# Edge aggregation on one core: 5 of the 17 edge tiles of a group multiplied whole in fp32

## The chip, the cores and the metric

The kernel runs on one core of one Trainium2 chip. The metric is the device time of one execution in microseconds (us). Engines are named as the profile names them: PE is TensorE, DVE VectorE, ACT ScalarE, POOL GpSimd, SP SyncE. A name with a q behind it (ACTq) is that engine's sequencer, the part that loads registers, branches, waits for semaphores and issues DMAs.

## The reference

Two GraphSAGE layers over a graph of 6250 nodes, 100000 edges (sorted by target `dst`) and 512 features, then a mixture of 8 experts with the best 2 for each node:

```python
def _sage_layer(h, src, dst, W_self, W_neigh, b, n_nodes):
    agg = segment_sum(h[src], dst, num_segments=n_nodes)
    deg = segment_sum(ones_like(dst), dst, num_segments=n_nodes)
    h_neigh = agg / maximum(deg, 1.0)[:, None]
    return relu(h @ W_self + h_neigh @ W_neigh + b)

h = _sage_layer(_layernorm(x), src, dst, W_self1, W_neigh1, b1, n)     # layer 1
h = _sage_layer(h, src, dst, W_self2, W_neigh2, b2, n)                 # layer 2
x = x + h
x = x + moe(_layernorm(x))                    # top 2 of 8 experts, 512 -> 512 -> 512
```

## The kernel before

**Stages.** First x is normalized into HBM (`xn_scratch`, about the first 108 us), and beside that DVE and PE make small tables from the edge list (`tables`, `in_order`, `tables2`, `tables3`). Then come layer 1, layer 2 and the experts.

**A layer.** The edges stand in 784 tiles of 128 edges (782 with real edges; `ET`, `TT`). POOL issues one indirect DMA for each tile (`gather`, L685) that fetches the 128 source rows into one of 28 slots of `store_all`. The nodes are done in 49 groups of 128. A group steps through 17 edge tiles (`ST`), k = 0 to 16, that start at its first tile; a tile that holds edges of two groups is stepped through in both. The rest of a group, seldom there, runs in an inner loop (k = 17). The sum over edges is a product with a 0/1 matrix: `sel` (edges x nodes of the group, built by DVE for three tiles at a time, L1232) times the rows.

**The split.** The rows are fp32 and are multiplied as two fp32r products. ACT rounds them to fp32r (`half`, L834, writes `r_hi`), DVE subtracts (`other_half`, L1240, writes `r_lo`), and PE multiplies `sel` by both (`sums`, L1646 and L1647); in layer 1 a third, 2 columns wide, counts the degree (L1645). `r_hi`, `r_lo` and `sel` are rings of 6 tiles: ACT and DVE wait for PE's semaphore `seg` before they write into a ring place again (`free_at`).

**Order.** `layer` writes the same order of steps on PE, ACT and DVE: before step k the pieces in `hooks[k]` are done, which belong to the node work of the group before or the one before that. On PE these are the 8 dense pieces of 3 matmuls at k = 0, 2, ... 14 (L1619), transposes at 3 and 11, and in layer 2 also transposes at 5, logits at 9, the list product at 13 and prefix sums at 17. On ACT `relu` (layer 1, L902) stands at 17 and waits for the last dense piece. In 32 of the groups of layer 1 (4 to 35) ACT also moves the experts' weights: `store_split` at 17 (L874), `load_raw` at 0 (L868). At the start of each group every engine loads its table entries into registers (`value`, L375): `tab_tile` on all three, and `tab_pos` on ACT alone (`places`).

**Slots.** SP passes on the arrival of each gather (`arrived`, L571). Every fourth tile it also waits until DVE's count `lo` (tiles whose `r_lo` is done) has passed the tiles 17 to 20 back (`freed`, L581), and then frees 4 slots; POOL waits for that before the gather that goes into them (L582 names it in the profile).

**Unsorted edges.** Where the tables find that the edges are not sorted (`loose`), every group goes over all 784 tiles again (`tab_laps`, `tab_pos`). With this input that path is not taken, but its table work and its loads are done.

## Time and profile before

| what | value |
|---|---|
| median of 3 runs | 3189.15 us (3183.64 to 3189.4) |
| profiled execution: own time / span | 3192.86 us / 3191.1 us |
| PE busy, weight loads busy | 2713.7 us (85%), 2108.6 us (66%) |
| DVE, ACT, POOL busy | 2280.9 (71%), 1727.3 (54%), 2189.5 us (69%) |
| granted PE clock, mean of the span | 0.904 |
| layer 1, from the first gather to the first of layer 2 | 108.9 to 1260.5 us |
| layer 2, to the end of its gathers | 1260.5 to 2371 us |

The span is what the profile shows between the first and the last instruction; the execution's own time is 1.8 us more. A busy share is an average over stages with different limits, and the ends of matmuls are modelled, so two matmuls in a row overlap in the rows; the distance between their starts is what one costs.

### The profile page before, as it was taken

How to read it: one execution, taken by the hardware profiler on the slowest of the kernel's cores; microseconds unless marked ns; L12 is line 12 of the kernel's file. 1: busy time of each engine (PE TensorE's matmuls, PEld its weight loads, DVE VectorE, ACT ScalarE, POOL GpSimd, SP SyncE). 2: the span in 40 equal slices, each digit the busy share in tenths (PEclk: the TensorE clock that was granted, in tenths of full speed). 3: DMA queues.
4: the chain of work that ended last, by engine and by line, in shares of the span. 5: the costliest groups of instructions: out<-in, count | busy, mean ns of one | idle time of the engine just before them, and what ended most of it. 6: DMA issues, size and time to landing. Idle time of an engine off the chain costs nothing.

```text
span 3191.1 us, 66577 instructions
## 1 busy us (share of the span) xinstructions
PE 2713.7 (85%) x12191; PEld 2108.6 (66%) x12192; DVE 2280.9 (71%) x5226; ACT 1727.3 (54%) x3193; POOL 2189.5 (69%) x2216
## 2 busy tenths in 40 slices
PE   1488878887889987899999999999996999899997
PEld 0366666666667765677777677777774777777775
DVE  7567666766667775888888888888875666666665
ACT  3455545545556654655656566555553555555554
POOL 0577777777777776777777777777753556555665
PEclk9988888888889998989899899888887999999998
DMA  7788888778877776777777777777765554555443
GB/s 276 230 256 267 270 273 268 254 254 267 257 247 227 213 215 222 231 231 231 235 236 234 234 230 234 227 233 224 235 196 157 136 135 75 132 133 135 73 80 63
DMA packets 234835, 664.22 MB, mean 208 GB/s; under 512 B 46602, under 2 KB 48196, under 8 KB 227612
## 3 DMA queue, kind: packets, MB, share of 16 engines
q0 software_dynamic: 151712, 465.58, 52.3%
q10 hardware_dynamic: 60768, 127.43, 11.2%
q1 hardware_dynamic: 22300, 70.69, 6.1%
q14 instruction: 46, 0.38, 0.0%
q8 instruction: 9, 0.15, 0.0%
HBM read 551.72 MB, written 111.83 MB: 208 GB/s over the span
## 4 chain that ended last, share of the span: by engine, by line
PE 36%; POOL 28%; issue 12%; DMA 11%; ACTq 5%; DVE 4%; ACT 2%; SPq 2%; DVEq 1%; POOLq 0%
POOL store_all L685 27%; PE ps L1619 22%; PE ps L1646 6%; DMA store_all<-h_scratch,srcT 5%; PE ps L1647 4%; ACTq L375 2%; DMA out<-store_all,idx_s 2%; DMA store_all<-xn_scratch,srcT 2%; DVE r_lo L1240 1%; PE ps L1747 1%; PE ps L1759 1%; DMA m_g<-gate_scratch,idx_g 1%; ACT r_hi L834 1%; ACTq L874 1%; ACTq L868 1%
## 5 line engine op out<-in xcount | busy, mean ns | idle before, releaser
L834 ACT ACTIVATE r_hi<-store_all 128x512 fp32r x1680 | 1008.0, 626 | 747.0 <-SPq L571 406.0
L1240 DVE TENSOR_TENSOR r_lo<-store_all,r_hi 128x512 fp32r<-128x512 f32 x1680 | 1130.2, 687 | 344.7 <-ACT r_hi L834 339.7
L685 POOL DMA_INDIRECT store_all<-xn_scratch,srcT x784 | 863.2, 1101 | 274.1 <-issue 227.4
L685 POOL DMA_INDIRECT store_all<-h_scratch,srcT x784 | 872.8, 1113 | 254.2 <-issue 239.3
L1646 PE MATMUL ps<-r_hi,sel 128*128 128x512 f32 x1680 | 831.0, 495 | 94.9 <-DVE r_lo L1240 94.0
L1647 PE MATMUL ps<-r_lo,sel 128*128 128x512 f32 x1680 | 711.2, 423 | 0.0
L1646 PEld LDWEIGHTS ps<-r_hi,sel 128*128 128x128 f32 x1680 | 348.4, 207 | 229.7 <-DVE r_lo L1240 162.1
L1232 DVE TENSOR_TENSOR sel<-iota_g,dstT 128x384 fp32r (+4 forms) x602 | 317.9, 528 | 137.3 <-PE ps L1647 93.8
L1619 PE MATMUL ps<-wts,sT 128*128 128x512 f32 x1176 | 415.7, 469 | 0.0
L1647 PEld LDWEIGHTS ps<-r_lo,sel 128*128 128x128 f32 x1680 | 352.5, 210 | 21.7
L1645 PEld LDWEIGHTS ps<-ones_col,sel 128*128 128x128 f32 x840 | 173.5, 206 | 286.7 <-issue 155.1
L1619 PE MATMUL ps<-wts,m_hT 128*128 x1224 | 326.4, 417 | 27.8 <-DVE m_hT L1496 23.3
L1645 PE MATMUL ps<-ones_col,sel 128*128 128x2 f32 x840 | 164.3, 196 | 209.2 <-DVE r_lo L1240 208.6
L1619 PE MATMUL ps<-wts,aT 128*128 128x512 f32 x1176 | 336.4, 395 | 0.0
L1619 PEld LDWEIGHTS ps<-wts,sT 128*128 128x128 f32 x1176 | 257.6, 227 | 86.8 <-issue 29.7
L1619 PE MATMUL ps<-wts,m_xT 128*128 x1224 | 311.6, 403 | 2.6 <-DVE m_xT L1486 2.5
L1619 PEld LDWEIGHTS ps<-wts,m_hT 128*128 128x128 f32 x1224 | 231.8, 196 | 98.4 <-issue 47.4
L1619 PEld LDWEIGHTS ps<-wts,m_xT 128*128 128x128 f32 x1224 | 223.2, 189 | 49.9 <-issue 3.4
L1619 PEld LDWEIGHTS ps<-wts,aT 128*128 128x128 f32 x1176 | 220.3, 188 | 52.6 <-DVE aT L1263 0.5
L953 ACT ACTIVATE store_all<-ps,b1T 128x128 f32<-128x128 f32 x408 | 116.7, 369 | 238.1 <-PE ps L1759 238.1
L743 POOL DMA_INDIRECT out<-store_all,idx_s x102 | 165.4, 1622 | 109.3 <-DMA store_all<-xn_scratch,idx_x 90.7
L730 POOL DMA_INDIRECT store_all<-xn_scratch,idx_x x104 | 105.6, 1015 | 121.4 <-PE ps L1747 87.2
(283 smaller groups left out, 3120.3 us busy)
## 6 DMA issues: line engine op xcount, KB each, us to landing
expert_weights_scratch<-w_both ACTq DMA_DIRECT2D x64, 512.0 KB, 5.2
wts<-expert_weights_scratch SPq DMA_DIRECT2D x32, 1024.0 KB, 10.3
store_all<-in_L_ffn_W ACTq DMA_DIRECT2D x64, 256.0 KB, 5.4
self_t<-xn_scratch ACTq DMA_DIRECT2D x49, 256.0 KB
store_all<-xn_scratch,srcT POOLq DMA_INDIRECT x784, 3.9
h_scratch<-x_t ACTq DMA_DIRECT2D x49, 256.0 KB
self_t<-h_scratch ACTq DMA_DIRECT2D x49, 256.0 KB
store_all<-h_scratch,srcT POOLq DMA_INDIRECT x784, 4.0
```

Of the source, the lines that this page charges most:

```text
L375: return eng.value_load(cell, min_val=0, max_val=top)
L685: pool.indirect_dma_start(rows[:, t % SLOTS, :], None, rows_d, bass.IndirectOffsetOnAxis(ap=srcT[:, t:t + 1], axis=0)).then_inc(s_rows[t % ...
L730: pool.indirect_dma_start(m_x, None, xn2_d, bass.IndirectOffsetOnAxis(ap=idx_x[:, 0:1], axis=0)).then_inc(M["x"], 16)
L743: pool.indirect_dma_start(out, bass.IndirectOffsetOnAxis(ap=idx_s[:, 0:1], axis=0), m_y, None, compute_op=ALU.add).then_inc(M["scat"], 16)
L834: act.activation(r_hi[:, ring(k), :], slot_of(t), ACT.Copy) \
L953: i = act.activation(m_hr[:, k, :], mhT_p[:, k * P:(k + 1) * P], ACT.Relu, bias=bias)
L1232: dve.tensor_tensor(sel[:, a:a + w, :], of_tile(g).unsqueeze(1).to_broadcast([P, w, P]), dstT[:, bass.ds(t, w)].unsqueeze(2).to_broadcast( ...
L1240: dve.tensor_tensor(r_lo[:, ring(k), :], slot_of(t), r_hi[:, ring(k), :].bitcast(F32), ALU.subtract).then_inc(S["lo"] if k < ST else S["lo ...
L1619: i = pe.matmul(out_ap, lhs[:, a, k, :], w[:, b, k, :], start=start and k == chunks[0] and (a, b) == (0, 0), stop=stop and k == chunks[-1] ...
L1645: pe.matmul(deg_of(g), sel[:, a, :], ones_col[:], start=k == 0, stop=False)
L1646: pe.matmul(agg_of(g), sel[:, a, :], r_hi[:, a, :], start=k == 0, stop=False)
L1647: pe.matmul(agg_of(g), sel[:, a, :], r_lo[:, a, :], start=False, stop=False) \
```

## The change

- `WHOLE = (2, 5, 8, 11, 14)`: for these 5 of the 17 steps ACT makes no `r_hi` and DVE no `r_lo`. PE multiplies `sel`, read as fp32, by the gathered rows in their slot as one fp32 matmul. It waits for `sel` (new semaphore) and for the arrival of the rows (`arr`). The inner loop (k = 17) stays split. The counts of `hi` and `lo` go by 12 tiles a group.
- Slots are freed by PE's `seg` (tile multiplied) and not by DVE's `lo` (tile split).
- The path for unsorted edges is gone: `in_order`, the `loose` steps of `tables2`, `tab_pos`, `tab_laps`, one product and one transpose of PE. 782 gathers a layer are issued and not 784.
- The last group covers nodes 6144 to 6249 alone: its edges are looked for from 6144 on (`thr_lo`), and the rows it shares with the group before are not stored by it (`own_rows`).

```diff
+WHOLE = (2, 5, 8, 11, 14)
+NSPLIT = ST - len(WHOLE)
+NSEL = -(-ST // SELW)
...
-                if places:
-                    t0 = value(eng, cell(places, g), NT * ET)
...
-                sp.wait_ge(S["lo"], packed // PACK + lap * ST)
-                sp.wait_ge(S["lox"], packed % PACK + lap * (ET - ST) + 1)
+                sp.wait_ge(S["seg"], packed // PACK + RING)
+                sp.wait_ge(S["segx"], packed % PACK + 1)
                 sp.sem_inc(S["slot"], BATCH)
...
-                for t in range(ET):
+                for t in range(TT):
...
                 def half(k, g, x, t):
 
+                    if k in WHOLE:
+                        return
...
-                layer(act, half, hooks, tab_tile, places=tab_pos, loop_end=loop_end,
+                layer(act, half, hooks, tab_tile, loop_end=loop_end,
...
-                        dve.wait_ge(S["lo"], g * ST)
+                        dve.wait_ge(S["sel"], g * NSEL)
...
+                        if k < ST:
+                            built.then_inc(S["sel"], 1)
+
+                    if k in WHOLE:
+                        return
                     if k < ST:
-                        dve.wait_ge(S["hi"], g * ST + (k + 1))
+                        dve.wait_ge(S["hi"], g * NSPLIT + (split_no(k) + 1))
...
                 def sums(k, g, x, t):
                     a = ring(k)
 
+                    if k in WHOLE:
+                        pe.wait_ge(S["sel"], g * NSEL + (k // SELW + 1))
+                        alone(pe, S["arr"], t + 1)
+                        if l == 0:
+                            pe.matmul(deg_of(g), sel[:, a, :], ones_col[:], start=False, stop=False)
+                        pe.matmul(agg_of(g), sel[:, a, :].bitcast(F32), slot_of(t), start=False, stop=False) \
+                            .then_inc(S["seg"], 1)
+                        return
```

PE in layer 1, steps k = 1 and 2 of a group and the piece at 3 (s1_ is a semaphore of layer 1), before:

```order
L1645 MATMUL ps<-ones_col,sel 128x2 [waits s1_lo]
L1646 MATMUL ps<-r_hi,sel 128x512
L1647 MATMUL ps<-r_lo,sel 128x512
L1619 MATMUL ps<-wts,sT 128x512 x3
L1645 MATMUL ps<-ones_col,sel 128x2 [waits s1_lo]
L1646 MATMUL ps<-r_hi,sel 128x512
L1647 MATMUL ps<-r_lo,sel 128x512
L1666 MATMUL ps<-ident,agg_s 128x128 [waits s1_aggLo,s1_evac]
```

and the same place after the change (L1584 is the dense piece, L1639 the transpose):

```order
L1618 MATMUL ps<-ones_col,sel 128x2 [waits s1_lo]
L1619 MATMUL ps<-r_hi,sel 128x512
L1620 MATMUL ps<-r_lo,sel 128x512
L1584 MATMUL ps<-wts,sT 128x512 x3
L418 ISA [waits s1_sel]
L1609 MATMUL ps<-ones_col,sel 128x2 [waits s1_arr]
L1610 ISA
L1610 MATMUL ps<-store_all,sel 128x512
L1639 MATMUL ps<-ident,agg_s 128x128 [waits s1_aggLo,s1_evac]
```

Step 2 no longer waits for DVE's `lo`, and one matmul of 512 columns that reads the slot itself stands where two stood.

ACT in layer 1 in the loop that also moves the experts' weights, from the start of a group (`load_raw` is L868) to its first step, before:

```order
L375 TENSOR_LOAD tab_tile
L375 ISA x2
L375 REGISTER_ALU
L375 TENSOR_LOAD tab_pos
L375 ISA x2
L425 REGISTER_ALU [waits s_wset]
L868 ISA [waits s_wl]
L868 DMA store_all<-in_L_ffn_W 128x512 x2
```

and after the change, where `load_raw` is L856:

```order
L368 TENSOR_LOAD tab_tile
L368 ISA x2
L418 REGISTER_ALU [waits s_wset]
L856 ISA [waits s_wl]
L856 DMA store_all<-in_L_ffn_W 128x512 x2
```

The second register load, of `tab_pos`, is gone from ACT's start of a group.

## Rows read from the trace of the kernel before

**Rows 1.** Busy time by stretch: us, each engine (instructions), granted clock, DMA, GB/s.
```profile
228.00:986.00 758.00, 614.41 (x2684) 484.43 (x2684) 506.40 (x908) 396.68 (x687) 567.59 (x514) 0.85 0.82 263
986.00:1060.00 74.00, 71.23 (x346) 56.70 (x345) 59.93 (x112) 47.47 (x85) 57.85 (x54) 0.98 0.72 217
1290.00:2376.00 1086.00, 1005.96 (x4519) 776.58 (x4519) 909.62 (x2345) 639.75 (x1105) 849.72 (x763) 0.90 0.75 230
```

**Rows 2.** Line L1653, PE, one a group: ns min/median/max, first, last start.
```profile
L1653 PE MATMUL ps<-zero_row,zero x31: 245/245/348, 252.0 to 985.5; 2*128 2x2 f32 x31
...
L1653 PE MATMUL ps<-zero_row,zero x4: 245/245/245, 1003.6 to 1059.4; 2*128 2x2 f32 x4
...
L1653 PE MATMUL ps<-zero_row,zero x48: 266/266/368, 1309.8 to 2376.0; 2*128 2x2 f32 x48
```

**Rows 3.** The chain of waits, 490 to 510 us: start us, us, what.
```profile
495.98 0.71 PE ps L1619 x3
...
498.58 1.38 ACTq L375
...
500.29 0.62 ACTq L375
...
504.39 0.37 PE ps L1645
```

**Rows 4.** Waits, 229 to 986.5 us: who <- for whom, us, times, longest us.
```profile
PE ps L1645 <- DVE r_lo L1240: 143.0, 36, 5.3
```

**Rows 5.** Waits, 1290 to 2377 us.
```profile
ACT r_hi L834 <- SPq L571: 299.4, 381, 4.9
...
PE ps L1646 <- DVE r_lo L1240: 75.3, 121, 1.6
```

**Rows 6.** Register loads by line L375, 229 to 986.5 us: ns min/median/max.
```profile
L375 ACTq TENSOR_LOAD <-tab_pos x32: 272/666/970, 229.8 to 985.1; - x32
```

**Rows 7.** PE in order of time, layer 1: start us, us, what.
```profile
1011.61 0.16 PE L1645 MATMUL ps<-ones_col,sel 128*128 128x2 f32 x1
...
1012.18 0.17 PE L1645 MATMUL ps<-ones_col,sel 128*128 128x2 f32 x1
```

**Rows 8.** PE in order of time, layer 2.
```profile
2018.13 0.40 PE L1647 MATMUL ps<-r_lo,sel 128*128 128x512 f32 x1
...
2018.60 0.39 PE L1647 MATMUL ps<-r_lo,sel 128*128 128x512 f32 x1
```

**Rows 9.** PE in order of time, the table products.
```profile
56.55 2.77 PE L1612 MATMUL ps<-ident,need 112*1 112x112 f32 x14 [6.47 <-DVE need L1157]
```

**Rows 10.** PE in order of time, the first edge tiles.
```profile
123.96 0.63 PE L1647 MATMUL ps<-r_lo,sel 128*128 128x512 f32 x1
124.38 0.20 PE L1645 MATMUL ps<-ones_col,sel 128*128 128x2 f32 x1
```

**Rows 11.** Line L685, POOL, the gathers: ns min/median/max, first, last start.
```profile
L685 POOL DMA_INDIRECT store_all<-xn_scratch,srcT x784: 950/957/2684, 108.9 to 1243.8; - x196
L685 POOL DMA_INDIRECT store_all<-h_scratch,srcT x784: 950/963/2233, 1260.5 to 2370.6; - x196
```

**Rows 12.** DVE and POOL in order of time, 114 to 118 us.
```profile
114.95 4.49 DVE L393 TENSOR_TENSOR wts<-store_all,wts 128x2048 fp32r<-128x2048 f32 x2 [20.11 <-ACT wts L388]
115.39 2.68 POOL L685 DMA_INDIRECT store_all<-xn_scratch,srcT  x1 [0.30 <-issue]
```

**Rows 13.** Waits of SP's sequencer, 229 to 986.5 us.
```profile
SPq L581 <- DVE r_lo L1240: 270.6, 92, 8.2
```

**Rows 14.** Page part 5: busy us, mean ns of one, idle before.
```profile
L1240 DVE TENSOR_TENSOR r_lo<-store_all,r_hi 128x512 fp32r<-128x512 f32 x1680 | 1130.2, 687 | 344.7 <-ACT r_hi L834 339.7
...
L1232 DVE TENSOR_TENSOR sel<-iota_g,dstT 128x384 fp32r (+4 forms) x602 | 317.9, 528 | 137.3 <-PE ps L1647 93.8
```

**Rows 15.** DVE in order of time, table work.
```profile
50.70 0.23 DVE L1134 TENSOR_SCALAR lap_row<-iota,loose 1x49 f32<-1x49 f32 x1
...
51.71 0.51 DVE L1145 TENSOR_TENSOR ahead<-tid,ps 112x343 f32<-112x343 f32 x1
```

## What the change does to the time, forecast before it was run

> **What bounds the kernel now.** I read the busy time by stretch first [rows 1]. Layer 1 has two regimes. Up to 986 us PE is 81% busy at a granted clock of 0.85; from 986 to 1060 us it is 96% busy at 0.98. Layer 2 lies between, 93% at 0.90. POOL is busy 75 to 78% in all three, but each gather is followed by 0.30 us of its own sequencer [rows 12], so POOL has almost nothing left either: 0.96 + 0.30 = 1.26 us is the least a gather takes, and layer 2 spends (2370.6 - 1260.5) / 783 = 1.42 us on one [rows 11].
>
> The period of a group comes from the start of its closing matmul [rows 2]. Up to 986 us it is (985.5 - 252.0) / 30 = 24.45 us, from 1003.6 to 1059.4 it is 18.6 us, and in layer 2 (2376.0 - 1309.8) / 47 = 22.7 us. A group needs about 16 new tiles (782 / 49), so the gathers alone would ask for 16 x 1.42 = 22.7 us. That is layer 2 exactly: there ACT waits 299 us for arrivals [rows 5], the gathers bound it, and PE follows with 75.3 / 48 = 1.6 us of waiting for `r_lo` a group. The 18.6 us is what PE needs when tiles lie ready and the clock is up: the price of a group on PE.
>
> The long periods up to 986 us are neither. The chain of waits shows them [rows 3]: PE ends the last dense piece (495.98 + 0.71), ACT's `relu` follows, ACT issues the stores of the split weights, loads `tab_tile` (1.38 us) and `tab_pos` (0.62 us), issues the loads of raw weights, rounds tile 0, DVE subtracts, and only at 504.39 can PE start tile 0. For some 4.6 us of it PE stands (143.0 us in 31 groups) [rows 4]. Everything else in that period is PE going from tile 0 to the last dense piece without a pause. PE also pulls the gathers back: SP waits 270.6 us for the split tiles before it frees slots [rows 13]. So in this region, about 33 groups with those before 252 us, each microsecond of PE work between tile 0 and the last dense piece counts in full.
>
> **One whole tile on PE.** At full clock a tile of layer 1 takes 12.18 - 11.61 = 0.57 us from start to start [rows 7], of layer 2 2018.60 - 2018.13 = 0.47 us [rows 8]. For a 512-column fp32 matmul the trace has no row; the nearest are the 7 table products with 112 columns, which are recorded as 14 [rows 9]: an fp32 matmul is two passes in the record, each 0.18 to 0.20 us long, 1.6 to 1.8 ns a column. The split matmul beside it takes 124.38 - 123.96 = 0.42 us for 512 columns, 0.82 ns each, at the half clock (0.63 us long there, 0.40 in rows 8) [rows 8, 10]. So a pass of fp32 costs twice a column and there are two: four fp32r matmuls for two. At full clock that is 4 x 0.21 to 0.23 = 0.87 us for 0.46, +0.41 us a tile; at half clock +0.86 us. Lower bound: no more than the pair it replaces, 0. Upper bound: if the table products ran at full clock, 2 x 512 x 1.77 ns = 1.8 us, +1.35 us. I take +0.41, since PE had been idle for 6.5 us before them, and the split matmuls that start after an idle time run at half clock [rows 9, 10].
>
> **Layer 1 up to 986 us.** Whole tiles 2, 5, 8 and 11 stand between tile 0 and the last dense piece (at k = 14); tile 14 stands behind it, beside ACT's chain, and is free while ACT takes longer. Tile 2 comes right after the stall, at half clock. That is 0.86 + 3 x 0.41 = 2.1 us a group. Against it ACT's chain loses `tab_pos`: its median is 0.67 us in this stretch [rows 6], with the 0.2 us of register work behind it 0.87 us, say 0.9. Net +1.2 us, times 33: **+40 us**. It could be 0, if the shorter stall keeps PE's clock up (2.1 us less half of a colder time of 3 to 4 us, less 0.9), and +76, if two more of the whole tiles fall into half clock. What ACT and DVE save there (5 x 0.63 and 5 x 0.69 us a group) is hidden by PE.
>
> Slots are now freed when PE is done with a tile, not DVE, which runs up to 6 ring places ahead. While PE bounds it this shifts nothing, but at 986 us up to 5 fewer gathers are under way: +5 us (0 to 8).
>
> **Gathers.** Their median is 0.96 us and the longest 2.7 us [rows 11]. The row at 115.39 shows what stretches them: that gather began while DVE ran the first of two subtractions with both operands in SBUF (4.49 / 2 = 2.2 us each, so until 117.2), and ended 0.9 us behind it, 1.7 us later than a usual one [rows 12]. In layer 2 a gather loses 1.42 - 0.96 - 0.30 = 0.15 us, over 1566 gathers some 235 us. By busy time r_lo has 1130 / (1130 + 318) = 0.78 of it against `sel` [rows 14], 183 us, and 490 of the 1680 r_lo go: 53 us, 0.034 us a gather. Between 0 (nothing of it is r_lo's) and 0.05. This counts only where gathers bound: the last 184 of layer 1 (783 less those issued by 986 us), **-6 us**; two empty gathers less at the end of layer 1, 2 x 1.4 = **-3 us**.
>
> The Trainium skill, page "SBUF — State Buffer", section "Who interferes with whom", says otherwise: a VectorE instruction with two SBUF inputs holds up a GpSimd instruction that reads SBUF, not one that only writes, and `tensor_tensor` did not stall descriptor generation. By that rule the term of -6 us would be 0 and the gather-bound case below would lose its gain. The row at 115.39 speaks against it, 2.68 us where 0.96 is usual [rows 11, 12].
>
> **Layer 2.** PE gets 5 x 0.41 = 2.05 us more a group, 2.5 with the fifth of the time that it spends at half clock [rows 1]. It has 1.6 us of waiting to put it in [rows 5], and less waiting should give back some of the clock; each 0.01 of clock is about 0.2 us. 22.7 - 1.6 + 2.5 - 0.6 = 23.0 us, against gathers of 16 x (1.42 - 0.034) = 22.2. PE becomes the bound there, by +0.3 us x 48 = **+15 us**; between -30 (gather-bound, see below) and +45 (no clock given back).
>
> **Start.** The table steps that go stand in DVE's chain ahead of the first gather: 51.71 - 50.70 = 1.0 us for one run of six [rows 15], and about 12 more of 0.15 to 0.5 us; together **-3 us** (0 to -5, as loads of x may fill it). Loads, stores and experts: no term, PE bounds the experts and nothing there is changed. The stores of the last group are 22 rows shorter, nothing.
>
> **Sum.** +40 +5 -6 -3 +15 -3 = +48 us on the profiled execution's own 3192.86 us gives 3241. That execution lies 3.7 us above the median of the runs, 3189.15, so the forecast is 3189 + 48 = **3237 us**. Its own range is 3192 to 3285: the first term between 10 and 60 us and layer 2 between 0 and 40.
>
> **Rivals.**
>
> *The gathers stay the bound (faster).* With fewer waits PE's clock rises and 2 us a group fit in. The Trainium skill, page "TensorE: Matmul & The Clock Gate", section "Why this matters for your kernels", asks for TensorE to be busy without gaps to keep the full clock; rows 1 agree as far as 0.98 in the dense stretch. Then layer 2 follows the gathers, 784 x -0.034 - 3 = -30 us, layer 1 up to 986 us is even, its end -9 and the start -3: -42 us, 3147 us. Against it: in layer 2 PE needs 18.6 + 2.05 = 20.7 us at full clock, but there are also small matmuls (logits, prefix sums) after which rows of before show the clock down.
>
> *PE pays more (slower).* The clock gives nothing back and half of the whole tiles up to 986 us meet the half clock: 33 x (3.2 - 0.9) = +76, layer 2 +45, slots +5, the rest -12: +114 us, 3303 us. It decides from the point where PE's period in layer 2 passes 23.5 us. For it: the mean clock of 0.85 [rows 1] leaves three tenths of the time at half speed.
>
> *An fp32 matmul costs no more than the pair.* Then ACT's saving stays (-30), gathers give -30 and the rest -9: -69 us, 3120 us. Only the short width of the table products leaves room for it.
>
> *The change does nothing*, since gathers bound before and after and PE absorbs it: within 6 us of before. It needs the gains and the losses of the first case to cancel.
>
> **How the numbers follow.** Chances: the forecast 0.62, PE pays more 0.18, gathers bound 0.12, fp32 cheap 0.03, nothing 0.05. What can be told from no change is about 0.2%, 6 us: below 3183 is faster, above 3195.5 slower. The forecast and the case above it are slower but for 0.04 of the forecast's low end, 0.76; faster 0.15; the same 0.09. For 8 in 10 the range runs from 3170, which leaves out most of the two fast cases, to 3300, which leaves out the upper half of the dear one.
>
> **What would show it.** The whole matmul in two records of about 0.43 us from start to start at full clock; the period of a group up to the end of the weights' moving at 25.6 us, and in layer 2 at 23.0 with PE over 97% busy and ACT's waits for arrivals well below 299 us; the register load of `tab_pos` gone from the chain; gathers with a mean 0.03 us shorter; SP waiting for PE where it freed slots. The forecast is wrong if the period in layer 2 is 22.2 us or less, or if the records of the whole matmul are much shorter or longer than 0.43 us.

## The result and the profile after

The changed kernel took 3151.28 us (median of 4 runs, 3146.70 to 3156.34), the kernel before on the same chip 3187.41 us (4 runs): a ratio of 0.9885, interval 0.9869 to 0.9901. It is faster by 36 us; 3237 us and "slower" were forecast. The profiled execution took 3153.0 us, its span 3151.2 us, 39.9 us under that of before.

Where the 39.9 us came from is read from the closing matmuls (now L1626), one a group. Groups 5 to 35 are the early stretch of layer 1 (closing 4 to closing 35), closings 49 to 97 are layer 2:

```profile
L1626 PE MATMUL ps<-zero_row,zero x32: 245/245/348, 223.8 to 982.8; 2*128 2x2 f32 x32
...
L1626 PE MATMUL ps<-zero_row,zero x49: 265/266/267, 1286.4 to 2339.5; 2*128 2x2 f32 x49
```

Before, the same closings stood at 228.1, 985.5, 1289.5 and 2376.0 (two of them in [rows 2]). So the start gave 4.3 us, the early stretch lost 1.5 (757.5 to 759.0), closings 35 to 49 gave 0.4, **layer 2 gave 33.4** (1086.5 to 1053.1), and what follows gave 3.4. The last of these is not read as a gain: what follows layer 2 took between 811.7 and 816.2 us in the kernels of the table below, with no edit to it among e1 to e16. The early stretch, where +40 was forecast, didn't move; layer 2, where +15 was forecast, is the gain.

The stretches of [rows 1] after the change, by stretch: us, each engine (instructions), granted clock, DMA share, GB/s:

```profile
228.00:983.00 755.00, 656.15 (x2678) 470.73 (x2678) 414.64 (x753) 313.03 (x532) 534.87 (x507) 0.91 0.81 261
983.00:1060.00 77.00, 77.00 (x348) 56.02 (x348) 48.68 (x93) 37.26 (x65) 59.88 (x57) 1.00 0.73 220
1290.00:2340.00 1050.00, 1020.16 (x4510) 741.26 (x4508) 785.52 (x2105) 496.03 (x864) 803.87 (x758) 0.95 0.77 237
```

The granted clock rose from 0.85 to 0.91 and from 0.90 to 0.95. In layer 2 PE is 97% busy, yet it is not the bound. The chain of waits of layer 2 (start us, us, what) is one gather behind another, each with its 0.30 us of sequencer, for tens of microseconds on end:

```profile
2010.24 0.95 POOL store_all L687
2011.19 0.30 issue
2011.49 0.95 POOL store_all L687
2012.44 0.30 issue
```

ACT still waits for arrivals, less than the 299.4 us of [rows 5] (who <- for whom: us, times, longest us), and PE waits less for `r_lo`: its matmuls for `r_lo` (75.3 us in [rows 5]) are no longer among the longest waits, only its weight loads:

```profile
ACT r_hi L822 <- SPq L569: 218.4, 194, 5.8
...
PEld ps L1619 <- DVE r_lo L1208: 56.5, 94, 1.7
```

The gathers that set the pace are shorter. Of line L687 the page gives the count, the busy us and the mean ns (1113 for layer 2 before); the view of the line gives ns min/median/max, where [rows 11] had a longest one of 2233 ns:

```profile
L687 POOL DMA_INDIRECT store_all<-h_scratch,srcT x782 | 828.9, 1060 | 262.0 <-issue 225.9
```

```profile
L687 POOL DMA_INDIRECT store_all<-h_scratch,srcT x782: 949/956/1498, 1257.6 to 2323.7; - x196
```

The whole tile itself costs what was forecast. PE in order of time, layer 2 (start us, us, what): from the first of the two records of the fp32 matmul to the next operation it is 0.86 us, where a split tile of [rows 8] took 0.47. The second fence is the chain of waits of an early group: it has 0.97 us for a layer-1 tile with its degree matmul, where [rows 7] had 0.57:

```profile
1690.67 1.02 PE L1610 MATMUL ps<-store_all,sel 128*128 x2
1691.53 0.95 PE L1672 MATMUL ps<-wg_s,store_all 128*128 128x8 f32 x8
```

```profile
494.25 1.39 ACTq L368
495.67 0.15 ACTq L368
...
499.19 0.37 PE ps L1618
...
502.86 0.97 PE ps L1610 x2
```

The second load of [rows 3] is gone: one `L368` stands there. PE's wait for the first tile's `r_lo`, 143.0 us in [rows 4], is 99.7 us. SP waits for PE where it frees slots (299.1 + 125.4 us in the early stretch, against 270.6 for DVE in [rows 13]).

### The profile page after: what moved, and what is told of

Its sections match the earlier page's. It is cut to its first block, busy times and chain, and to the rows that moved or that the text cites. A ratio compares the mean times of both kernels' runs of the same rounds, so it can differ in the third digit from the quotient of the medians.

```text
span 3151.2 us, 64888 instructions
## 1 busy us (share of the span) xinstructions
PE 2786.8 (88%) x12188; PEld 2058.8 (65%) x12189; DVE 2007.8 (64%) x4721; ACT 1446.7 (46%) x2703; POOL 2109.5 (67%) x2212
## 3 DMA queue, kind: packets, MB, share of 16 engines
q10 hardware_dynamic: 60660, 127.29, 11.1%
## 4 chain that ended last, share of the span: by engine, by line
PE 48%; POOL 22%; issue 10%; DMA 9%; ACTq 4%; DVE 3%; ACT 2%; DVEq 1%; SPq 1%; POOLq 0%
PE ps L1584 24%; POOL store_all L687 22%; PE ps L1610 6%; PE ps L1619 6%; PE ps L1620 4%; DMA out<-store_all,idx_s 2%; DMA store_all<-h_scratch,srcT 2%; ACTq L368 1%; DVE r_lo L1208 1%; PE ps L1720 1%; PE ps L1732 1%; DMA m_g<-gate_scratch,idx_g 1%; DMA store_all<-in_x 1%; DMA store_all<-xn_scratch,srcT 1%; ACT r_hi L822 1%
## 5 line engine op out<-in xcount | busy, mean ns | idle before, releaser
L687 POOL DMA_INDIRECT store_all<-xn_scratch,srcT x782 | 824.3, 1054 | 304.3 <-issue 223.4
L822 ACT ACTIVATE r_hi<-store_all 128x512 fp32r x1190 | 721.3, 626 | 660.4 <-SPq L569 318.8
L687 POOL DMA_INDIRECT store_all<-h_scratch,srcT x782 | 828.9, 1060 | 262.0 <-issue 225.9
L1208 DVE TENSOR_TENSOR r_lo<-store_all,r_hi 128x512 fp32r<-128x512 f32 x1190 | 804.8, 687 | 303.6 <-ACT r_hi L822 301.5
L1619 PE MATMUL ps<-r_hi,sel 128*128 128x512 f32 x1190 | 582.4, 489 | 44.6 <-DVE r_lo L1208 44.1
L1610 PE MATMUL ps<-store_all,sel 128*128 x980 | 540.4, 634 | 0.0
L1620 PE MATMUL ps<-r_lo,sel 128*128 128x512 f32 x1190 | 493.8, 415 | 0.0
L1584 PE MATMUL ps<-wts,sT 128*128 128x512 f32 x1176 | 424.9, 474 | 0.0
L1584 PE MATMUL ps<-wts,aT 128*128 128x512 f32 x1176 | 374.7, 427 | 0.0
L1584 PE MATMUL ps<-wts,m_hT 128*128 x1224 | 327.1, 418 | 23.8 <-DVE m_hT L1464 20.7
L1619 PEld LDWEIGHTS ps<-r_hi,sel 128*128 128x128 f32 x1190 | 238.8, 201 | 156.3 <-DVE r_lo L1208 81.9
L1584 PEld LDWEIGHTS ps<-wts,sT 128*128 128x128 f32 x1176 | 240.7, 212 | 113.8 <-issue 70.8
L1584 PE MATMUL ps<-wts,m_xT 128*128 x1224 | 312.1, 404 | 2.5 <-DVE m_xT L1454 2.5
L1584 PEld LDWEIGHTS ps<-wts,m_hT 128*128 128x128 f32 x1224 | 232.9, 197 | 93.9 <-issue 42.2
L1584 PEld LDWEIGHTS ps<-wts,aT 128*128 128x128 f32 x1176 | 221.2, 188 | 88.7 <-issue 45.8
L1618 PEld LDWEIGHTS ps<-ones_col,sel 128*128 128x128 f32 x595 | 118.7, 199 | 221.8 <-issue 129.6
L1620 PEld LDWEIGHTS ps<-r_lo,sel 128*128 128x128 f32 x1190 | 242.0, 203 | 24.1 <-issue 9.4
L1584 PEld LDWEIGHTS ps<-wts,m_xT 128*128 128x128 f32 x1224 | 224.0, 190 | 49.6 <-issue 3.4
```

The source lines that it names most:

```text
L687: pool.indirect_dma_start(rows[:, t % SLOTS, :], None, rows_d, bass.IndirectOffsetOnAxis(ap=srcT[:, t:t + 1], axis=0)).then_inc(s_rows[t % ...
L822: act.activation(r_hi[:, ring(k), :], slot_of(t), ACT.Copy) \
L1208: dve.tensor_tensor(r_lo[:, ring(k), :], slot_of(t), r_hi[:, ring(k), :].bitcast(F32), ALU.subtract).then_inc(S["lo"] if k < ST else S["lo ...
L1584: i = pe.matmul(out_ap, lhs[:, a, k, :], w[:, b, k, :], start=start and k == chunks[0] and (a, b) == (0, 0), stop=stop and k == chunks[-1] ...
L1610: pe.matmul(agg_of(g), sel[:, a, :].bitcast(F32), slot_of(t), start=False, stop=False) \
L1618: pe.matmul(deg_of(g), sel[:, a, :], ones_col[:], start=k == 0, stop=False)
```

## The experiments

Each stretch below is read from the closings of the kernel's own trace, the gathers from its page. "Early" is closings 4 to 35, "layer 2" closings 49 to 97. Each ratio is to the kernel before on the same chip. The ratios are of medians, the other columns of one profiled execution each, which lies up to 6 us from its kernel's median (e8: 14 us above it). How far a stretch varies where nothing in it was changed is seen in e1, e5 and e6, whose layer 1 is the same: 743.9, 738.2 and 741.4 us in the early stretch, and 1053.8, 1050.6 and 1055.4 us from closing 4 to 49. Differences of under 6 us between single stretches are not read as effects.

| kernel | ratio (interval) | early, us | layer 2, us | gather in layer 2, mean / longest ns |
|---|---|---|---|---|
| before | 1 | 757.5 | 1086.5 | 1113 / 2233 |
| the change | 0.9885 (0.9869 to 0.9901) | 759.0 | 1053.1 | 1060 / 1498 |
| e1, no whole tile | 0.9981 (0.9969 to 0.9992) | 743.9 | 1093.9 | 1120 / 2236 |
| e2, TensorE's part alone | 1.0037 (1.0022 to 1.0053) | 767.0 | 1092.2 | 1112 / 2232 |
| e3, relief without price | 0.9830 (0.9805 to 0.9855) | 750.7 | 1050.2 | 1061 / 1891 |
| e4, change + load | 1.0075 (1.0053 to 1.0096) | 811.9 | 1052.3 | 1064 / 1500 |
| e5, layer 2 only | 0.9857 (0.9838 to 0.9877) | 738.2 | 1052.7 | 1063 / 1499 |
| e6, seven in layer 2 | 0.9947 (0.9931 to 0.9964) | 741.4 | 1082.7 | 1023 / 1480 |
| e7, two-input filler | 1.0011 (1.0001 to 1.0021) | 763.8 | 1094.0 | 1114 / 2238 |
| e8, one-input filler | 1.0003 (0.9991 to 1.0015) | 766.7 | 1098.8 | 1125 / 2007 |
| e13, ScalarE kept busy | 0.9907 (0.9890 to 0.9924) | 766.1 | 1052.2 | 1063 / 1499 |
| e14, small filler | 0.9860 (0.9845 to 0.9874) | 757.7 | 1055.9 | 1064 / 1497 |
| e15, e1 + slots by `r_lo` | 0.9966 (0.9954 to 0.9978) | 740.7 | 1087.3 | 1112 / 2234 |
| e16, e1 + load | 1.0015 (1.0005 to 1.0025) | 757.8 | 1093.6 | 1120 / 2252 |

**e1, no whole tile.**

```
-WHOLE = (2, 5, 8, 11, 14)
+WHOLE = ((), ())          # one list a layer
```

> The change without its whole tiles: all 17 edge tiles of a group are split again, in both layers; the freed slots, the shorter tables, the removed position load and the removed path stay. Two theories of the 36 us that the change gained. Theory R (relief): with five r_lo fewer in a group, VectorE holds up fewer gathers, they stay the bound of layer 2 and are shorter, and TensorE's extra time fits beneath. Then the whole tiles bring nearly all of it: this run takes 3180 to 3190 us, its layer-2 period is 22.6 to 22.8 us and a gather lasts 1.10 us again. Theory L (load): the terms of the forecast for the removed load (33 groups x 0.9 us) and for the start hold, and it is they that paid: this run takes 3150 to 3160 us, with the early groups at 23.0 us instead of 23.9. The third, theory C (clock), says that the denser TensorE gives half-clock time back: this run is then near 3185 us too, but with half-clock time in layer 2 again at 4 to 5 us a group.

3186.81 us, ratio 0.9981. All else of the change is worth 6 us, the whole tiles some 30 (0.9981 to 0.9885). Theory L falls: the 14 us won in the early stretch (757.5 to 743.9) are lost again later (closings 35 to 49: 304.0 to 309.9 us, layer 2 +7.4). Layer 2 is slow again with long gathers. Its rows (closings; then the two stretches, as above):

```profile
L1626 PE MATMUL ps<-zero_row,zero x49: 266/266/369, 1278.2 to 2372.1; 2*128 2x2 f32 x49
```

```profile
224.40:968.30 743.90, 628.47 (x2683) 497.07 (x2683) 510.76 (x908) 399.01 (x687) 573.71 (x512) 0.86 0.83 267
...
1278.20:2372.10 1093.90, 1021.82 (x4521) 794.20 (x4520) 910.66 (x2347) 638.29 (x1106) 852.48 (x760) 0.88 0.75 228
```

**e2, TensorE's part alone.** The early returns for whole tiles are taken out on ScalarE and VectorE; PE waits for an `r_lo` that it doesn't read.

```
                     if k in WHOLE:
                         ...
+                        pe.wait_ge(S["lo"], g * ST + k + 1)
                         ...
                         pe.matmul(agg_of(g), sel[:, a, :].bitcast(F32), slot_of(t), start=False, stop=False) \
```

> The five tiles are multiplied whole on TensorE, but ScalarE and VectorE still make r_hi and r_lo for all 17 (the five halves are made and not used), so no engine but TensorE is changed by the whole tiles. Theory R: no relief, the gathers stay at 1.10 us and the layer-2 period at 22.7 us or above, TensorE pays what it can't hide: 3185 to 3230 us. Theory C: the fuller TensorE keeps its clock without any relief: 3150 to 3170 us, layer-2 period near 22.0 us.

3207.81 us, ratio 1.0037: slower than before, in theory R's range. Layer 2 took 1092.2 us, as without whole tiles, so nothing is gained (theory C falls, as the cause of the gain), and nothing is lost either: PE took in the five whole tiles. The rows show how:

```profile
227.50:994.50 767.00, 663.58 (x2682) 474.02 (x2683) 510.51 (x908) 401.74 (x687) 548.56 (x512) 0.91 0.81 259
...
1300.60:2392.80 1092.20, 1046.81 (x4521) 747.04 (x4520) 908.27 (x2347) 637.28 (x1106) 846.94 (x761) 0.95 0.76 229
```

In layer 2 PE's 240 whole tiles cost 240 x 0.39 = 94 us at full clock. PE's busy time rose by 25 us only (1021.8 to 1046.8), while the granted clock rose from 0.88 to 0.95, so some 69 us came back from the clock. The other kernels that split all tiles (before, e15, e16) have 1006.2 to 1011.1 us at 0.89 to 0.90; against them it is 36 to 41 us more and 53 to 58 back. In the early stretch the price is 31 groups x 5 x 0.40 = 62 us, and PE's busy time rose by 35 us at a clock of 0.91 instead of 0.86: at most 27 us came back there, and the stretch lengthened by 23 us.

**e3, relief without price.**

```
-                        pe.matmul(agg_of(g), sel[:, a, :].bitcast(F32), slot_of(t), start=False, stop=False) \
+                        pe.matmul(agg_of(g), sel[:, a, :], slot_of(t).bitcast(F32R), start=False, stop=False)
+                        pe.matmul(agg_of(g), sel[:, a, :], slot_of(t).bitcast(F32R), start=False, stop=False) \
```

This kernel leaves out the rest of the rows (`r_lo`) and counts them twice in these tiles; it serves for the time alone.

> The other half: ScalarE and VectorE are spared the five tiles as in the change, but TensorE multiplies the row itself twice in fp32r (as long as a split tile takes; the sums of these five tiles come out doubled), so TensorE pays nothing. Theory R: the relief alone is the gain, the whole tiles' price was hidden in layer 2 and partly paid in layer 1: 3120 to 3150 us, layer-2 period 21.9 us as with the change, TensorE idle more. Theory C: without a fuller TensorE the clock falls again, and the time is above the change's, 3160 to 3185 us, with 4 to 5 us at half clock in a layer-2 group.

3143.23 us, ratio 0.9830. The relief alone has the whole gain of layer 2 (1050.2 us) at a clock of 0.91. So a higher clock isn't what gains; it is what pays for the whole tiles.

**e4, the load again.**

```
                 packed = value(eng, cell(table, g), ET * PACK + ET)
                 ...
+                if last == 2:              # ScalarE in layer 1
+                    value(eng, cell(tab_extra, g), NT * ET)
```

> The change, with one more register load for each group on ScalarE where the removed position load stood (of the table of further tiles, its value unused). The forecast's term says 0.9 us a group in the early region of layer 1, some 30 us in all: 3175 to 3185 us. If the load stood beside other waits there it costs under 0.2 us a group: 3148 to 3156 us.

3218.47 us, ratio 1.0075, some 61 us above the change (0.0190 x 3193). The early stretch took 811.9 us, 52.9 more, 1.7 us a group; the forecast had 0.9. The chain of waits of an early group (start us, us, what): the second load and its register work put 1.3 us between the first and everything behind:

```profile
514.83 0.94 ACTq L368
515.80 0.15 ACTq L368
516.10 0.94 ACTq L368
517.06 0.15 ACTq L368
517.60 0.36 ACTq L858
```

The stretch's clock fell from 0.91 to 0.87 with it. PE waits 33.6 us longer for the first tile (99.7 to 133.3 us), and its busy time is 20 us longer (657.4 to 677.7).

```profile
225.50:1037.40 811.90, 677.66 (x2683) 482.99 (x2683) 416.52 (x753) 313.46 (x531) 539.30 (x511) 0.87 0.77 244
```

**e5 and e6, layer 2 only; seven tiles.** `WHOLE` becomes one list a layer.

```
+WHOLE = ((), (2, 5, 8, 11, 14))          # e5
+WHOLE = ((), (2, 4, 6, 8, 10, 12, 14))   # e6
```

> The five whole tiles in layer 2 alone; layer 1 splits all 17. Theory R (relief, pays where the gathers set the pace): layer 2 keeps its 1053 us (closings 49 to 97, against 1094 us without whole tiles), and layer 1 no longer pays for the whole tiles: its end stands as without them, 8 us earlier than with the change. That gives 3140 to 3148 us at this chip's pace of the first runs. If the layers weren't separate (layer 1's whole tiles also pay), it is at the change's 3151 us or above.

3147.64 us beside 3196.80 of before, 0.9857. Layer 2 keeps its gain (1052.7 us), and layer 2 begins 11.1 us earlier than with the change (1275.3 against 1286.4). The intervals of the two ratios overlap, so that it beats the change by some 9 us is likely, not shown by the medians.

> Seven whole tiles (2, 4, ..., 14) in layer 2, none in layer 1. Theory R gives 8.2 us for each r_lo spared in layer 2 (41 us for five) as long as TensorE fits beneath: a group at full clock is 20.46 us with five, 21.3 us with seven, and the gathers' pace would be 21.6 us: 3124 to 3132 us. If the gathers' gain is no longer had (TensorE sets the pace once waits and some half-clock time are added), the layer stays at 1050 us or above and the time at 3140 us or above.

3178.54 us, 0.9947: the second case. The gathers are shorter still (1023 ns), but POOL now waits 55.0 us for slots (11.9 with the change), SP waits for PE where it frees them, and PE is busy for 98% of layer 2 at 0.95; seven whole tiles make it the bound. The stretch, and SP's waits in it:

```profile
1278.70:2361.40 1082.70, 1059.56 (x4522) 747.07 (x4521) 732.10 (x2011) 450.22 (x771) 777.79 (x761) 0.95 0.76 231
```

```profile
SPq L578 <- PE ps L1620: 409.3, 95, 9.3
...
SPq L578 <- PE ps L1610: 152.4, 45, 7.0
```

**e7 and e8, fillers on VectorE.**

```
                     if k in WHOLE:
+                        dve.wait_ge(s_fixed, g * len(WHOLE) + (l * NT * len(WHOLE) + WHOLE.index(k) + 1))
+                        dve.tensor_tensor(fixed[:, 1], fixed[:, 0], fixed[:, 0], ALU.subtract).then_inc(s_fixed, 1)
                         return
```

and in e8, in place of the last added line:

```
+                        dve.tensor_scalar(fixed[:, 1], fixed[:, 0], 1.0, None, ALU.add).then_inc(s_fixed, 1)
```

> The change, but VectorE does for each whole tile, in the place of the r_lo that it is spared, a subtraction of the same size with two inputs in SBUF, of a constant (its result isn't used). ScalarE and TensorE stay as changed. If it is VectorE's two-input operations that hold up the gathers, the relief is gone: layer 2 at 1085 to 1100 us, a gather at 1.10 us, 3185 to 3205 us. If it is ScalarE's r_hi that was the load on them, or only that VectorE and ScalarE free their buffers sooner, it stays at 3150 to 3160 us.

3199.19 us, 1.0011; layer 2 at 1094.0 us, gathers at 1114 ns. VectorE's work is the cause, as expected.

> As the run before, with an operation that reads one input (a constant plus 1.0, same 128x512 size) in place of the subtraction. If the gathers are held up by two-input operations alone, this one costs next to nothing: 3148 to 3160 us, a gather at 1.05 to 1.06 us, layer 2 at 1053 us. If any work of VectorE on SBUF holds them up, it is as slow as with the subtraction, in proportion to its length.

3197.89 us, 1.0003; layer 2 at 1098.8 us. This is against what I expected: a filler with one input, 0.44 us long (0.69 for the other), costs as much. So "two inputs" is not the whole of it. The profiled execution is the slowest of its 12, 14 us above the median, so its layer 2 may be some us too long; the ratio says the same without it.

**e9 to e12 and e17, e18: two slower chips.** Six kernels fell on two chips where the kernel before itself took 3801 and 3783 us, not 3193 to 3197. In layer 2 of the change there (e17) POOL waited for free slots for 313.5 us, where it waited for 11.9 on the first chip (POOL's waits: us, times, longest us):

```profile
POOL store_all L687 <- SPq L579: 313.5, 100, 11.0
POOL store_all L687 <- issue: 200.6, 647, 1.0
```

The DMA engines moved 185 GB/s in that stretch there, 237 on the first chip. Why is open: these traces don't say when a gather landed. Another thing than the gathers' issue bounds there (layer 2 took 1321 to 1341 us in all six), so four of them were repeated (e13 to e16). Their edits and those of the repeats are the same.

> The change, but ScalarE makes for each whole tile a copy of the size of an r_hi, of a constant (not used), behind the same two waits; VectorE stays relieved. Theory V: the gain of layer 2 is VectorE's alone: layer 2 stays at 1050 to 1060 us and the time at 3148 to 3162 us. If ScalarE's relief carried part of it, layer 2 rises toward the 1092 us of the run with both halves kept.

3698.36 us, ratio 0.9756 (0.9706 to 0.9807).

> The run with VectorE's one-input filler cost layer 2 as much as the two-input one (1099 and 1094 us), against what I expected. This one has the same 490 fillers on 32 columns instead of 512. Theory O (occupancy: what counts is how long VectorE works without a hole, since a gather that starts in a hole is not held): a filler of some 100 ns gives most of the gain back, layer 2 at 1053 to 1065 us, 3150 to 3170 us in all. Theory I (one more instruction with its wait between the r_lo shifts what each gather meets, whatever its length): layer 2 stays at 1085 us or above.

3681.76 us, 0.9721 (0.9667 to 0.9775).

> No whole tiles, and the slots are freed by r_lo (before TensorE has multiplied) as in the kernel before, not by TensorE. The forecast's term says that freeing by TensorE costs 5 us, all of it in the early groups of layer 1: this run is then 5 us below the one without whole tiles, at 0.9965 of before. If later freeing costs nothing, as layer 2 suggests (no wait for slots there), it is within 2 us of it, 0.998.

3747.74 us, 0.9850 (0.9778 to 0.9921).

> No whole tiles, and the extra register load on ScalarE again: near to the kernel before in all but the freed slots. The load cost 62 us beside the whole tiles, where the forecast had 0.9 us for each of 33 groups. If the load's price depends on the whole tiles (TensorE's later r_hi), it is far cheaper here, 10 to 30 us: 1.001 to 1.008 of before. If it is the load itself (1.27 us of ScalarE's queue ahead of the copy of the sums in each early group), it costs 50 us or more here too: 1.013 or above.

3650.13 us, 0.9627 (0.9577 to 0.9677): the fastest of the six, with no whole tile and one load too many. None of the four forecasts came true there, and none of these runs answers its question. For the last pair see the end of this section.

**e13, ScalarE kept busy.** In `half`, for a whole tile, behind the same waits:

```
+                        act.activation(fixed[:, 1], fixed[:, 0], ACT.Copy).then_inc(s_idle, 1)
```

> The kernel with ScalarE kept busy (a copy of a constant for each whole tile, VectorE relieved), again, since the last call's chip had slow transfers (before at 3801 us; the gathers no longer set the pace alone). Theory V, VectorE's relief alone pays: layer 2 at 1050 to 1060 us, ratio to before 0.988 to 0.991. If ScalarE's relief carries part of it: layer 2 toward 1092 us, ratio above 0.994.

3165.39 us, 0.9907; layer 2 at 1052.2 us. The gain of layer 2 is VectorE's alone. The early stretch is 7 us longer (766.1 against 759.0), little more than it varies by; that ScalarE's work does it is not shown.

**e14, small filler.** As e8, on 32 columns (0.19 us).

> The filler of 32 columns on VectorE, again. Theory O (occupancy): layer 2 at 1053 to 1065 us, ratio 0.988 to 0.993. Theory I (an instruction more, whatever its length): layer 2 at 1085 us or above, ratio 0.998 or above.

3152.27 us, 0.9860; layer 2 at 1055.9 us. These fillers' number and waits don't matter; how long VectorE works does. Theory O's forecast came true, though between 0.19 us (no cost) and 0.44 us (the whole cost) nothing was tried.

**Why a gather is held.** The traces of e1 and e8 say what e8 left open. VectorE and POOL in order of time in layer 2, first of e1, then of the change (start us, us, what):

```profile
2011.89 0.48 DVE L1352 TENSOR_SCALAR w_both<-iota_c,col_f,idcode 128x400 fp32r<-128x400 f32 x1
2012.04 2.23 POOL L687 DMA_INDIRECT store_all<-h_scratch,srcT  x1 [0.30 <-issue]
2012.29 0.56 DVE L1196 TENSOR_TENSOR sel<-iota_g,dstT 128x384 fp32r x1
2012.76 0.69 DVE L1208 TENSOR_TENSOR r_lo<-store_all,r_hi 128x512 fp32r<-128x512 f32 x1
```

```profile
2011.49 0.95 POOL L687 DMA_INDIRECT store_all<-h_scratch,srcT  x1 [0.30 <-issue]
2011.58 0.69 DVE L1208 TENSOR_TENSOR r_lo<-store_all,r_hi 128x512 fp32r<-128x512 f32 x1
...
2015.01 0.68 DVE L1208 TENSOR_TENSOR r_lo<-store_all,r_hi 128x512 fp32r<-128x512 f32 x1
...
2015.26 1.25 POOL L687 DMA_INDIRECT store_all<-h_scratch,srcT  x1 [0.30 <-issue]
```

A gather that begins in a hole of VectorE takes 0.95 us, even if an `r_lo` begins 0.09 us behind it: of 494 such gathers in both layers of the change one was held. One that begins inside an `r_lo` ends 0.82 us behind its end (2015.69 to 2016.51). Of 500 that began inside an `r_lo`, 369 took over 1.00 us. What is left of the `r_lo` decides: with 0.2 us or more left 347 of 368 were held, with less than 0.13 us none of 57. That is the usual 0.95 less the 0.82: the place in the issue where it is held lies some 0.13 us behind its start (an estimate from these rows).

An unbroken row of operations doesn't hold a gather to its end as such. In the change a gather that begins inside `sel`, with an `r_lo` right behind, ends 0.82 us behind `sel` (2018.67 to 2019.49):

```profile
2018.11 0.56 DVE L1196 TENSOR_TENSOR sel<-iota_g,dstT 128x384 fp32r x1
2018.22 1.27 POOL L687 DMA_INDIRECT store_all<-h_scratch,srcT  x1 [0.31 <-issue]
2018.58 0.68 DVE L1208 TENSOR_TENSOR r_lo<-store_all,r_hi 128x512 fp32r<-128x512 f32 x1
```

So did all 134 that were held of the 187 that began that way, and all 65 held of 66 that began in an `r_lo` with another behind. The long ones begin inside an operation with one input, `w_both` in the rows of e1, with `sel` and `r_lo` right behind, and end 0.82 us behind the `r_lo`: 2.23 us. All 38 over 1.9 us in layer 2 of e1 are of this kind; of the 48 with e8's kernel 17 are, and 31 begin where the filler and a short `place_i` end:

```profile
2003.09 0.42 DVE L1208 TENSOR_SCALAR fixed<-fixed 128x512 f32<-128x512 f32 x1
2003.42 0.16 DVE L1338 CAST place_i<-place 128x2 int32<-128x2 f32 x1
2003.47 2.00 POOL L689 DMA_INDIRECT store_all<-h_scratch,srcT  x1 [0.30 <-issue]
2003.49 0.55 DVE L1200 TENSOR_TENSOR sel<-iota_g,dstT 128x384 fp32r x1
2003.96 0.68 DVE L1214 TENSOR_TENSOR r_lo<-store_all,r_hi 128x512 fp32r<-128x512 f32 x1
```

Why a gather that begins in the operation ahead is held through two, and one that begins in the first of the two only through one, stays open.

The last column of the table splits the kernels in two by the long ones: 1.5 us where five or seven `r_lo` are spared without a long filler (1.9 in e3), 2.0 or more elsewhere. Gathers over 1.9 us number 38 in layer 2 of e1, 26 before, 32 with e2's and e7's kernels each and 48 with e8's; there is none in layer 2 of the change and none with the small filler.

By what runs when the held gather begins, the time above 0.953 us of gathers over 1.00 us in layer 2 is:

| begins inside | e1 | the change | e7 | e8 |
|---|---|---|---|---|
| `r_lo` | 69.0 | 55.4 | 49.3 | 50.5 |
| `sel` | 6.3 | 25.9 | 6.1 | 39.5 |
| the filler | | | 25.8 | 4.0 |
| others (the long ones) | 52.2 | 0.1 | 42.6 | 36.4 |
| all gathers | 128.2 | 82.1 | 124.7 | 132.7 |

From e1 to the change that is -46 us, and layer 2 is 40.8 us shorter. The filler of e8 holds hardly a gather itself; the time comes back through `sel` and the long ones. Where the gathers begin among VectorE's operations moves with the filler, and which part of the gain is VectorE's shorter work and which this shift was not separated.

**e15 and e16, the small terms of layer 1.** From e1: `wait_ge(S["lo"], ...)` in place of `S["seg"]` where SP frees slots (e15), and the load of e4 (e16).

> No whole tiles, slots freed by r_lo, again. If freeing by TensorE costs the 5 us of the forecast in the early groups: ratio 0.9965 and groups 5 to 35 in 739 us (744 without whole tiles and with slots freed by TensorE). If it costs nothing: 0.998 and 744 us.

3184.33 us, 0.9966 against 0.9981: 5 us by the medians, with overlapping intervals. But it isn't where the forecast had it. The early stretch of 740.7 us lies among the 738.2 to 743.9 of the kernels that free by PE, and both kernels reach closing 49 at the same time (1278.6 and 1278.2 us). The difference is in layer 2, 1087.3 against 1093.9 us, where SP waits for either engine for under 1 us. All five kernels with long gathers that free by PE take 1092.2 to 1098.8 us there, the two that free by `r_lo` 1086.5 and 1087.3. Why is open.

> No whole tiles, the extra load on ScalarE, again. If the load's price depends on the whole tiles: groups 5 to 35 in 755 to 775 us, ratio 1.001 to 1.008. If it is the load itself, as dear as beside the whole tiles (53 us in these groups): 790 to 800 us, ratio 1.013 or above.

3202.06 us, 1.0015: 11 us more than e1, and the early stretch is 13.9 us longer. Without whole tiles the load costs 0.45 us a group, beside them 1.7. So neither has a price of its own: in the early stretch whole tiles cost 54 us with the load there (757.8 to 811.9) and 15 without it (743.9 to 759.0). PE's wait for the first tile grows by the same amount both times, 33.8 us (112.6 to 146.4) and 33.6 us in e4, 1.1 us a group. What differs is PE's busy time: 17 us less here (628.5 to 611.4), 20 us more there.

**e17 and e18, the change beside a likely better version.** e18 is e5 with the slots of layer 1 freed by `r_lo`.

> The change itself, beside the next run on one chip: 0.987 to 0.990 of before, layer 2 (closings 49 to 97) at 1053 us.

3688.62 us beside 3782.66, 0.9761 (0.9718 to 0.9804).

> Whole tiles in layer 2 alone, and the slots of layer 1 freed by r_lo as before. If the prices of layer 1 are real (8 us less without the whole tiles up to closing 49, 3 to 5 us less with slots freed by r_lo), it stands 8 to 14 us below the change beside it, 0.983 to 0.986 of before, with layer 2 at 1053 us still. If they were noise between chips, the two are within 3 us.

3754.22 us, 0.9932 (0.9890 to 0.9974): on this chip it is slower than the change, by 92 us in the early stretch (952.9 against 860.4). On both such chips the kernels that free the slots of layer 1 by `r_lo` took 947.1 and 952.9 us there, the others 855.8 to 884.6. Why the earlier release is worse on these chips stays open, and so does whether e18 is the better one on the other chips.

## Why the prediction was wrong

**What held.** Gathers set the pace of layer 2 before. A whole tile costs 0.39 to 0.40 us more. The start: the first gather of an edge tile begins at 105.7 us instead of 108.9, -3 forecast. The place of the stall, and that ACT's chain carries it. That `r_lo` holds gathers. The Trainium skill, page "SBUF — State Buffer", section "Who interferes with whom", says that `tensor_tensor` did not stall descriptor generation. Here 347 of 368 gathers that began with 0.2 us or more of an `r_lo` ahead were held; by the same section two SBUF inputs hold up a GpSimd instruction that reads SBUF, and these gathers do read a tile there, `srcT`, so that half of it agrees.

**The step that failed first: layer 2, +15 us.** It took PE's added 2.5 us a group, put 1.6 into waiting and let the clock give back 0.6, so that PE became the bound at 23.0 us. The price of a whole tile at full clock was right. What it adds to PE's busy time was not: 2.5 - 0.6 = 1.9 us a group in the sum, 25 / 48 = 0.5 in e2 against e1 (0.8 against e16 and before), since the clock rose from 0.88 to 0.95. With that the sum gives 22.7 - 1.6 + 0.5 to 0.8 = 21.6 to 21.9 us, under the gathers' 22.2, and PE is not the bound. So the case called "the gathers stay the bound" is what happened. "The forecast is wrong if the period in layer 2 is 22.2 us or less": it is 1053.1 / 48 = 21.9.

That case had 3147 us, and 3151 was measured; in part that is luck. Its layer 2 (-30, measured -33.4), its early stretch (0, measured +1.5) and its start are right. Its -9 for the end of layer 1 is not seen against before (-0.4), and 3.4 us come from what follows layer 2, which the change doesn't touch.

I had the row for it. A fifth of layer 2's time at half clock is not a surcharge on the new work, as "2.5 with the fifth of the time that it spends at half clock" has it; fuller work draws on it. The Trainium skill, page "TensorE: Matmul & The Clock Gate", section "Why this matters for your kernels", asks for TensorE to be kept busy without gaps, and the trace agrees: 0.90 before at 93% busy, 0.95 after at 97%. I gave that rival 0.12.

**Gathers, sized by share.** -0.034 us a gather came from an even share of `r_lo` in the holding; it was 0.053 (0.060 from e1), with e1's and the change's sums above: the direct holding by `r_lo` fell by 13.6 us, the long ones by 52 us, while `sel` took 20 more. The long ones depend on what runs where a gather begins, and no proportion gives that; e8 shows that the loss comes back whole with 0.44 us of other work.

**Layer 1 up to 986 us, +40 us.** The term was 33 x (2.1 - 0.9): +69 for whole tiles, -30 for the load. Between the same versions the runs show +15 (e1 to the change; 15 to 21 with e5 and e6 in e1's place) and -14. The mis-sized part of the first is the 2.1 us, with each added microsecond of PE counted in full: PE's busy time rose by 29 us, 0.9 a group (628.5 to 657.4), and its wait for the first tile fell by 13 (112.6 to 99.7). The load was sized rightly as a wait, which fell from 143.0 to 112.6 us, the 30 us forecast; but PE's busy time rose by 15 us meanwhile (613.8 to 628.5), against the step that everything else in the period stays. The two terms share one stall and don't add: with the load in place the whole tiles cost +54. The clock fell with the load from 0.91 to 0.87 beside whole tiles and from 0.86 to 0.85 without; that the longer stall keeps it down, and so makes the whole tiles dear, is argued, not shown.

**Slots +5, empty gathers -3, layer 1's last gathers -6.** The 5 us for the slots are not seen at 986 us: e1 and e15 reach closing 49 together. The whole tiles did shorten closings 35 to 49 by 6.3 us (309.9 to 303.6), as forecast for the last gathers, but that stretch had become 5.9 us longer without them (304.0 to 309.9, e1), which no term had. None of these decided anything.

**Two slips in the sums.** The forecast's own range, from 10 to 60 us and 0 to 40, ends at 3237 + 20 + 25 = 3282, not 3285. And two more whole tiles at half clock make 2.1 + 2 x 0.45 = 3.0 us a group, so that the +76 of the dear case (with 3.2) is +69. Neither changes the account.

## What to carry to other kernels

When an engine with a variable clock is near its bound, count its time at half clock as room: price added work at the full clock against waits plus half of the half-clock time, before calling it the new bound. Not all of that room is to be had: here the clock stopped at 0.95 with PE 96 to 98% busy (e2, the change, e6), and with seven whole tiles PE was the bound. When a gather's issue sets the pace, look for its longest ones and what VectorE runs beneath them: here taking work off VectorE paid in a jump, not in proportion. Terms that share a stall are to be measured together, since either one's price depends on the other.

## What the runs showed of the hardware

- An fp32 matmul of 512 columns takes 0.86 us at full clock, in two records (0.43 us apart in the row of layer 2 above).
- In the change's layers a gather's issue was held, with one exception in 494, only if it began while VectorE ran an operation. `r_lo` and `sel`, with two inputs in SBUF, held it where 0.2 us or more of them was left (347 of 368, 154 of 196); it then ended 0.82 to 0.84 us behind that operation's end (1.25 and 1.27 us in the rows above). None was held of 63 that began inside a subtraction with one input in PSUM (`sT`), nor of 52 that began inside the batch-norm operations, which read one tile in SBUF.
- A gather that began in a short operation with one input, with `sel` and `r_lo` right behind, was held to the end of both (2.00 and 2.23 us).
- On two of the five chips of the experiments the same kernel took 3783 and 3801 us, not 3193 to 3197, and edits changed their order there (e12, e18).
